# Moving the maximum of x up one slot and dt times x down one slot on VectorE

## The reference

```python
u  = silu(conv3(x));  B, C = split(u @ W_bc + b_bc);  dt = softplus((u @ W_dt + b_dt) @ W_dtp + b_dtp)
dA = exp(A * dt);  dB = B * u_in * dt       # u_in is x; 16 states for each of 128 features
h[t] = dA[t] * h[t-1] + dB[t];  y[t] = sum_n C[t, n] * h[t, n]
x1 = layernorm(x + y + x * D)               # the layer's own skip is x * D
hid = silu(fp4(x1) @ fp4(w_gate).T) * (fp4(x1) @ fp4(w_up).T)      # inner width 352
out = layernorm(x1 + fp4(hid) @ fp4(w_down).T)
```

## Time and profile before

| | us |
|---|---|
| median of 3 runs (lowest, highest) | 379.6 (379.29, 380.64) |
| the profiled execution, its own time | 379.2 |
| its span | 377.4 |
| VectorE busy in the span | 326.5 (87%) |
| GpSimd busy | 279.3 (74%) |
| PE busy (matmuls, modelled ends) | 265.9 (70%) |
| ScalarE busy | 230.2 (61%) |

### The profile page before, as it was taken

One profiled execution on the slowest core, in us unless ns is written; L12 is line 12 of the kernel. 1 busy time (PEld: TensorE's weight loads), 2 busy tenths in 40 slices (PEclk: granted clock), 3 DMA queues, 4 the chain that ended last, 5 costly groups with the idle time before them and its releaser, 6 DMA issues.

```text
span 377.4 us, 4003 instructions
## 1 busy us (share of the span) xinstructions
PE 265.9 (70%) x1130; PEld 124.9 (33%) x1130; DVE 326.5 (87%) x365; ACT 230.2 (61%) x509; POOL 279.3 (74%) x167
## 2 busy tenths in 40 slices
PE   2657777678857887788778878787886691692881
PEld 1122222213311345233523343234322460361571
DVE  4873979899999999999899999999899997468970
ACT  3453773865586558965896589657964663154434
POOL 0092466669388999899989998999899999514642
PEclk9999898879987999999999999999999687596897
DMA  3750290073008300840074007500640000000001
GB/s 47 173 124 0 44 208 2 0 167 83 0 2 182 71 1 2 180 98 0 3 166 113 0 2 153 125 2 2 139 112 2 0 0 29 2 2 28 0 2 56
DMA packets 19246, 21.86 MB, mean 58 GB/s; under 512 B 6096, under 2 KB 15128, under 8 KB 19224
## 3 DMA queue, kind: packets, MB, share of 16 engines
q1 hardware_dynamic: 18504, 21.05, 24.6%
q10 hardware_dynamic: 720, 0.56, 0.8%
HBM read 2.72 MB, written 2.10 MB: 13 GB/s over the span
## 4 chain that ended last, share of the span: by engine, by line
POOL 25%; ACT 18%; PE 16%; DVE 16%; issue 14%; SPq 6%; DMA 3%; POOLq 0%; DVEq 0%; ACTq 0%
POOL product L758 8%; DVE states L1020 6%; SPq L440 5%; POOL qh_norm L779 4%; POOL qh_norm L774 4%; POOL hq L814 3%; DVE db L1004 3%; PE ps_prep L1316 3%; ACT ps_decay L483 3%; DMA dt_rep<-dtx 3%; ACT c_rep L559 2%; PE ps_prep L1303 2%; PE ps_y L1282 2%; ACT L552 2%; POOL rstd L768 2%
## 5 line engine op out<-in xcount | busy, mean ns | idle before, releaser
L758 POOL TENSOR_TENSOR product<-states,c_rep 128x1024 f32<-128x1024 f32 x63 | 148.7, 2367 | 37.8 <-DVE states L1020 36.3
L483 ACT ACTIVATE ps_decay<-dt_rep,aneg 128x512 f32<-128x512 f32 x128 | 87.0, 690 | 45.2 <-DVE states L1020 42.0
L1020 DVE TENSOR_TENSOR_SCAN states<-ps_decay,states,db 128x512 f32<-128x512 f32 x64 | 78.9, 1259 | 3.1 <-POOL product L758 3.1
L1004 DVE SCALAR_TENSOR_TENSOR db<-ps_b,bbc_rep,dt_rep 128x2048 f32<-128x2048 f32 x31 | 72.4, 2337 | 9.4 <-PE ps_b L1323 6.2
L1020 DVE TENSOR_TENSOR_SCAN states<-ps_decay,db 128x512 f32<-128x512 f32 x64 | 75.3, 1202 | 0.3
L1323 PE MATMUL ps_b<-u_feat,wbc_rep 128*128 128x512 f32 x64 | 38.3, 684 | 15.5 <-DVE db L1004 14.9
L1316 PE MATMUL ps_prep<-u_feat,wbc_rep 128*128 128x512 f32 x56 | 32.0, 654 | 16.9 <-ACT c_rep L559 16.8
L1282 PE MATMUL ps_y<-product,gather 128*32 128x512 f32 x256 | 37.4, 662 | 2.6 <-POOL product L758 2.4
L1348 PE MATMUL ps_f<-gate_t,xq_t 128*128 128x352 f32 x56 | 24.5, 519 | 12.4 <-DVE hidden L1070 8.3
L594 ACT ACTIVATE gate_tanh<-ps_f 128x352 f32<-128x352 f32 x28 | 13.0, 465 | 27.6 <-PE ps_f L1348 27.6
L559 ACT ACTIVATE c_rep<-ps_prep,bbc_rep 128x512 f32<-128x512 f32 x28 | 19.4, 692 | 13.1 <-PE ps_prep L1316 12.4
(11 more groups left out here) (202 smaller groups left out, 518.8 us busy)
## 6 DMA issues: line engine op xcount, KB each, us to landing
dt_rep<-dtx SPq DMA_DIRECT2D x124, 128.0 KB, 2.4
x_tok<-in_L_attn_x SPq DMA_DIRECT2D x8, 256.0 KB, 3.0
out<-y_out SPq DMA_DIRECT2D x8, 256.0 KB, 2.3
dt_rep<-dtx ACTq DMA_DIRECT2D x4, 128.0 KB, 3.7
hidden<-in_L_ffn_w_down SPq DMA_DIRECT2D x1, 176.0 KB, 3.4
x_feat<-in_L_attn_x SPq DMA_DIRECT2D x8, 0.5 KB, 2.6
hidden<-in_L_ffn_w_gate SPq DMA_DIRECT2D x1, 128.0 KB, 3.2
hidden<-in_L_ffn_w_up SPq DMA_DIRECT2D x1, 128.0 KB, 3.0
```

The costliest lines, as they stand in the source:

```text
L483: nc.scalar.activation(ps_decay[BANK_OF[k]][:], dt_rep[p][:, c, 0, :], ACT.Exp, scale=aneg[:, c, m:m + 1]).then_inc(decay_done, 1)
L758: nc.gpsimd.tensor_tensor(product[:, j % PRODUCTS], states[p][:, first:first + 2, :], over(c_rep[p][:, j // SET_PAIRS, :], 2), ALU.mult).t ...
L1004: nc.vector.scalar_tensor_tensor(out=db[m % DB][:], in0=over(ps_b[:], QUADS), scalar=bbc_rep[:, 0, m:m + 1], in1=dt_rep[p][:, :, 1, :], op ...
L1020: nc.vector.tensor_tensor_scan(out=states[p][:, k % ring, :], data0=ps_decay[BANK_OF[k]][:], data1=db[k // QUADS % DB][:, k % QUADS, :], i ...
```

## The change

Two entries of the table change: `dtx` goes from behind the scan of slot 6 to behind the scan of slot 7; maximum and scale of x go from behind the scan of slot 7 to behind the scan of slot 6; the reciprocal keeps its place between the scans of slots 7 and 8, but now belongs to slot 7 and so stands ahead of `dtx`.

```diff
-    "dve u": 4, "dve dtx": 6, "dve tiles": 15,
-    "dve x quant": {0: (7, False), 1: (7, False), 2: (8, True), 5: (10, False)},
+    "dve u": 4, "dve dtx": 7, "dve tiles": 15,
+    "dve x quant": {0: (6, False), 1: (6, False), 2: (7, False), 5: (10, False)},
```

## The result

The changed kernel takes 389.0 us (387.91 to 389.8), the kernel before 379.62: ratio 1.0246, 95% interval 1.0199 to 1.0293. Beside each other on another chip the two gave 388.9 and 379.49, ratio 1.0214 (1.0172 to 1.0257). The profiled execution took 387.91 us with a span of 386.1, 8.7 us more than the span before; it was the quickest of the four.

What follows compares the result with a forecast made beforehand. A loop of `dtx`, 12.9 us of transfer, `db` and VectorE's work was taken to bound the kernel. 1.13 + 13.92 - 4.77 - 0.7 - 0.1 = 9.5 us more gave a median of 389.0 us, range 385.5 to 391.5.

Steps and rivals of the forecast that it cites:

- The ring: `dtx`, 12.9 us of transfer, `db`, VectorE's work to the scan of slot 6, `dtx` again; chance 0.78.
- The argument for the ring: Seven `dtx` to `db` distances of 12.86 to 13.40 us, with differing work between, were taken to pin the transfer.
- What comes into the ring: Scan of slot 7, maximum, scale and reciprocal now stand ahead of `dtx`: 2.32 us a unit.
- What goes: VectorE's idle before `dtx`, 4.77 us in five units, is filled.
- The rival of the late softplus: ScalarE's chain is pushed back too, so idle at `dtx` stays beside the new one at `db`: 393.8 us; chance 0.10.
- The pass over h beside GpSimd: VectorE's bf16 pass (L964) may wait 0.3 us longer, covered ahead of `db`: nothing, or 1.8 us if uncovered.
- The sum: Over the whole kernel, 1.13 + 13.92 - 4.77 - 0.7 - 0.1 = 9.5 us slower.
- the transfer is hidden anyway: Rival: `db` could start 10.6 us after `dtx`, so only idle goes: 374.8 us, faster; chance 0.04.
- only the three named waits are real: Rival: only three `db` waits on DMA are real, the four other equal distances coincidence: about 385 us; chance 0.08.

Runs made afterwards that it cites:

- after12: Changed kernel with the last quarter's four of 16 transfers left out from unit 2 on: 379.24 us, ratio 1.0006 to the kernel before.
- after_actq: Changed kernel with the last two of a unit's 16 transfers issued by ScalarE instead of SyncE: 383.36 us, ratio 1.0086 to the kernel before.
- before20: Kernel before with four useless small transfers added ahead of the last quarter of units 1 to 7: 391.47 us against 379.81, ratio 1.0309.
- before12: Kernel before with the last quarter's four of 16 transfers left out from unit 2 on: 378.66 us, ratio 1.0022.
- dtx_only: Kernel before with only `dtx` moved from slot 6 to 7, the quantisation of x left in place: 388.36 us against 378.77, ratio 1.0287.
- x_only: Kernel before with only maximum, scale and reciprocal of x moved up, `dtx` left in slot 6: 379.23 us against 378.77, ratio 1.0028.
- after20: Changed kernel with the four useless small transfers added ahead of the last quarter of units 1 to 7: 409.6 us, 18.1 above before20.

## Why the prediction was right

*The ring.* Right for the changed kernel. `dtx` to `db` stayed at 12.8 to 13.5 us, the wait moved from `dtx` to `db`, all seven `db` wait for dt_rep<-dtx, unit 0's by 3.04 us (3.0 was written) and the others by 1.96 to 2.70. A unit takes 39.0 to 39.4 us, for the 39.2 to 39.5 written. Shown from three sides: with a shorter transfer the loss is gone (after12), with a somewhat shorter one more than half is (after_actq), with a longer one the kernel before is slower by about what the ring says (before20).

*The argument for the ring* was weaker than it looked. I took the seven equal distances for a sign that the transfer sets them although the work between differs. In before12 the transfer is shorter and the distances are still 12.6 to 13.0 us, by VectorE's own work. In the kernel before, too, VectorE arrived at its last six `db` 12.65 to 13.00 us behind `dtx`, if the wait is taken off. There transfer and work happened to be about equally long, and either would have given equal distances. Better evidence was the first pair of the earlier trace rows, where VectorE arrived after 10.98 us and stood 1.88 for the transfer, and the sum of issues and landing. before20 and the changed kernel then showed it.

*What comes into the ring.* 2.32 us was taken; 2.18 is what it took. The scan starts 0.11 us behind the start of the scale, where the reciprocal had started 0.23 behind; perhaps because the scan does not need the scale's result, which no run tests. Six times 0.14 is 0.8 us too much.

*What goes.* The 4.77 us of idle before `dtx` went in full, and so did 0.7 us of waits for products. The softplus was 2.1 us early in the step shown, and no `dtx` had idle ahead of it. The rival of the late softplus did not happen in any unit.

*The pass over h beside GpSimd.* It took 0.92 us instead of 0.56, so 0.36 longer, for the 0.3 expected; the wait for the transfer hid it. GpSimd's timeline of the changed kernel has the operation beside it:

```profile
198.73 1.06 POOL L787 TENSOR_TENSOR qx_norm<-x,qx_inv 128x512 f32<-128x512 f32 x1
```

The pass began at 199.26, the GpSimd operation ended at 199.79, and the pass 0.39 later. That is the rule of the Trainium skill (SBUF — State Buffer, Who interferes with whom) that was weighed in the prediction; the trace agrees. In dtx_only, where the distance between the two engines is another, the pass took 0.50. In x_only it took up to 1.22.

*The sum.* 9.5 us was forecast, 9.48 is the lateness of the last `db` in the first trace, and by medians the change cost 9.4 us on both chips (389.0 against 379.62, 388.9 against 379.49). That exactness is in part luck. 1.13 + 6 x 2.18 - 4.77 - 0.7 - 0.1 = 8.6 is the sum with the measured stretch. In the first trace the head was 1.9 us early and `u_feat` 2.6 us late, which left 0.6 on top, and the landings differ by a tenth here and there. The span of that trace grew by 8.7 us only, since the stretch behind the last `db` was 0.8 shorter; in the second trace of the changed kernel the last `db` came at 286.20, 7.9 us later than before. So single traces scatter by more than the 0.8 us by which the term was too large. In the medians something made up for those 0.8 us; TensorE's clock may have, as below, but no run separates it.

*The rivals.* That the transfer is hidden anyway falls by the 16.6 us of waits. That only the three named waits are real falls by before20 and by the four later units, in each of which `db` now waits some 2 us.

*What I left out* is TensorE's clock: a longer standstill at `db` makes TensorE stand too. Behind the 2.23 us of wait at 209.47 TensorE had stood 1.47 us and its matmul pair for B took 1.12 us, as at the upper level. But in dtx_only one such pair ran at the lower level behind a standstill of about the same length, 1.52 us:

```profile
171.01 2.07 PE L1323 MATMUL ps_b<-u_feat,wbc_rep 128*128 128x512 f32 x2 [1.52 <-DVE db L1004]
```

`hidden` then waited 0.44 us for the tanh. So a standstill of that length has a price in some steps and none in others. Over whole executions the mean granted clock is 0.89 in the changed kernel and 0.87 in after20, where the kernel before has 0.90 to 0.91 beside them. The prediction put nothing for this, and how much of the 9.4 us it is stays open.

## What to carry to other kernels

Before filling the idle time ahead of an instruction, look at what starts behind it: here a chain of 16 issues and a landing that somebody waits for, and the right place for the producer was as early as possible, idle or not. Add up issues and landing, and compare them with the distance from the producer to the waiting instruction. Equal distances in several places are no proof: the engine's own work may be as long as the transfer, as before12 shows here. Make the transfer longer or shorter by a few issues to see whether the time follows. If it does, price a move by what passes ahead of the producer less the idle that it fills. Filling the idle brought nothing in this kernel, with the transfer as it was or two issues shorter.

## What was not expected of the hardware

Moving two of 16 issues from SyncE to ScalarE brought 0.6 us on average and not 1.3: beside ScalarE's two, SyncE's 14 took 0.63 to 0.68 us each (0.63 in most steps of the kernel before), and the landings took 2.6 to 3.1 us instead of 2.4. The Trainium skill (DMA: Bandwidth & Descriptors, Rules for kernel authors) says that spreading transfers over several issuing engines saves only the sequencer's issue time; in after_actq only about half of that time was saved.

And a wait on VectorE has a second price on TensorE: behind 3.81 us of standing the granted clock was 0.54 for some 7 us, and a matmul pair of 1.0 to 1.1 us took 2.08. In after20 `hidden` waited 3.3 us more for the tanh than in before20, which is most of the 3.9 us above the ring's sum.
